# One more weight tile looked up on TensorE in the step loop of a one-core transformer layer

## The reference, cut to what matters

```
H, I, CS, CB = 1024, 2752, 8, 16384
Wg, Wu, Wd = codebook[idx_gate], codebook[idx_up], codebook[idx_down]   # (I,H), (I,H), (H,I)
g = einsum('bsh,ih->bsi', x, Wg)
u = einsum('bsh,ih->bsi', x, Wu)
out = einsum('bsi,hi->bsh', silu(g) * u, Wd)                            # x: (2, 1024, 1024)
```

## Time and profile before

| | us |
|---|---|
| median of 3 runs | 6918.13 |
| lowest and highest | 6914.07, 6921.35 |
| the profiled execution | 6914.47 |
| its span | 6912.6 |
| TensorE busy | 6672.6 (97%) |
| GpSimd busy | 5037.7 (73%) |
| VectorE busy | 4539.3 (66%) |
| ScalarE busy | 3665.4 (53%) |

### The profile page before, as it was taken

The page is one execution under the profiler, slowest core; times in us unless marked ns, Lnnn a source line. Parts: engine busy times, 40 slices in busy tenths (PEclk is TensorE's granted clock), DMA queues, the critical chain, the costliest instruction groups (busy, mean ns, idle before and its releaser), DMA issues.

```text
span 6912.6 us, 118754 instructions
## 1 busy us (share of the span) xinstructions
PE 6672.6 (97%) x29072; PEld 4082.8 (59%) x29072; DVE 4539.3 (66%) x11051; ACT 3665.4 (53%) x6498; POOL 5037.7 (73%) x5316
## 2 busy tenths in 40 slices
PE   9999999999999999999999999999999999999936
PEld 4444666666666566666666666666666666666513
DVE  3320778887777677776677766777767777677512
ACT  0000777776666555555555655555555555555401
POOL 7777777777777777777777777777777777777773
PEclk9999999999999999999999999999999999999968
DMA  4232111113333333333333333333333333333211
GB/s 139 61 89 47 33 34 34 34 34 89 81 84 82 62 67 73 72 73 73 67 74 73 73 74 73 66 73 74 73 73 67 77 73 72 74 68 73 59 13 51
DMA packets 472588, 463.19 MB, mean 67 GB/s; under 512 B 231248, under 2 KB 347728, under 8 KB 467536
## 3 DMA queue, kind: packets, MB, share of 16 engines
q10 hardware_dynamic: 287072, 396.63, 20.4%
q0 software_dynamic: 169984, 22.10, 7.8%
q1 hardware_dynamic: 14832, 36.84, 1.4%
HBM read 397.97 MB, written 57.15 MB: 66 GB/s over the span
## 4 chain that ended last, share of the span: by engine, by line
DMA 73%; issue 24%; POOLq 1%; POOL 1%; PE 1%; DVE 0%; ACT 0%; DVEq 0%
DMA raw<-in_codebook_dram,idx_sb 73%; POOLq L207 1%; POOL raw L208 1%; PE ps L465 0%; DVE small L1040 0%; PE ps L552 0%; ACT arena L845 0%; POOLq L196 0%; DVE small L1043 0%; DMA idx_sb<-in_idx_dram 0%; PE ps L545 0%; POOLq L217 0%; DVE small L1050 0%; DVE big L979 0%; ACT arena L729 0%
## 5 line engine op out<-in xcount | busy, mean ns | idle before, releaser
L208 POOL DMA_INDIRECT raw<-in_codebook_dram,idx_sb x5312 | 5037.5, 948 | 1796.1 <-DMA raw<-in_codebook_dram,idx_sb 1595.2
L987 DVE TENSOR_SCALAR_CACHE_REDUCE onehot<-arena,small 128x512 fp32r<-128x512 f32 x3685 | 2514.3, 743 | 1045.9 <-PE ps L419 998.6
L419 PE MATMUL ps<-onehot,table 128*128 128x512 f32 x11776 | 3123.7, 416 | 21.3 <-ACT onehot L757 17.7
L419 PEld LDWEIGHTS ps<-onehot,table 128*128 128x128 f32 x11776 | 2194.5, 188 | 864.6 <-issue 357.6
L753 ACT ACTIVATE onehot<-arena,small 128x512 fp32r<-128x512 f32 x2211 | 1434.3, 713 | 1113.9 <-PE ps L419 1076.6
L757 ACT ACTIVATE onehot<-onehot,small 128x512 fp32r<-128x512 f32 x2211 | 1425.3, 708 | 0.0
L447 PE MATMUL ps<-big,arena 128*128 128x512 f32 (+1 forms) x2816 | 1295.7, 597 | 124.3 <-DVE arena L971 123.4
L447 PEld LDWEIGHTS ps<-big,arena 128*128 128x128 f32 (+1 forms) x2816 | 515.5, 187 | 725.5 <-issue 577.1
L465 PE MATMUL ps<-arena 128*128 128x512 f32 (+1 forms) x1408 | 651.3, 599 | 2.1 <-ACT arena L729 1.1
L994 DVE SCALAR_TENSOR_TENSOR picked<-arena,small,ps 128x512 f32<-128x512 f16 x736 | 548.3, 745 | 153.3 <-PE ps L430 139.0
L979 DVE TENSOR_TENSOR big<-ps,big 128x512 f32<-128x512 f32 x704 | 486.3, 691 | 161.1 <-PE ps L465 151.4
(11 more groups left out here) (69 smaller groups left out, 2740.6 us busy)
## 6 DMA issues: line engine op xcount, KB each, us to landing
arena<-code_low ACTq DMA_DIRECT2D x738, 256.0 KB
arena<-code_high ACTq DMA_DIRECT2D x738, 128.0 KB
raw<-in_codebook_dram,idx_sb POOLq DMA_INDIRECT x5312
gathered_units<-raw SPq DMA_DIRECT2D x40, 512.0 KB
arena<-gathered_units ACTq DMA_DIRECT2D x20, 1024.0 KB
queries_keys<-arena ACTq DMA_DIRECT2D x16, 1024.0 KB, 4.0
arena<-queries_keys ACTq DMA_DIRECT2D x32, 512.0 KB
big<-in_xT_dram ACTq DMA_DIRECT2D x4, 2048.0 KB, 16.9
```

Source lines behind the costliest of these rows:

```text
L208: pool.indirect_dma_start(raw[:, s, n, :], None, codebook, bass.IndirectOffsetOnAxis(ap=idx_sb[:, s, n:n + 1], axis=0), engine_sem=describ ...
L419: last = mm(ps[:, 4 + s % 2, :], table[:, k, c, :], onehot[:, k, :], start=(k == 0 and c == 0), stop=(k == KLO - 1 and c == PIECES - 1))
L987: dve.tensor_scalar(onehot[:, k, :], lo_sb[:, s % 2, :], kp_sb[:, k:k + 1], None, ALU.is_equal, ALU.add, accum_out=hits[:, k:k + 1]).then_ ...
```

## The change

Down of tile 21 is looked up instead of gathered. NLOOK goes from 23 to 24 and the gathered units from 42 to 41; the step loop runs from 1 to 20 on every engine; behind it only gate, up and down of tile 21 are left, and the transposes of the gathered down weight go. The scratch areas for the codes are 3200 instead of 3072 wide. An index load for unit 41 is still issued, of zeros.

```diff
-NPK = NTILE - 1
-UNITS = 1 + 2 * (NTILE - 1) + 1
-PAIRS = (UNITS - 4) // 2
+UNITS = 1 + 2 * (NTILE - 1)
+PAIRS = (UNITS - 3) // 2
-NLOOK = 3 + NPK
+NLOOK = 3 + NTILE
@@ GpSimd
-            for s in range(2):
-                gather_unit(1, s, P, 16 * PAIRS + 32, 16 * PAIRS + 16, 2 * P * (PAIRS + 1) + (s * P - P + CS * CS))
+            gather_unit(1, 0, P, 16 * PAIRS + 32, 16 * PAIRS + 16, 2 * P * (PAIRS + 1) + (CS * CS - P))
@@ TensorE
-            with pe.Fori(1, NPK) as step:
+            with pe.Fori(1, NTILE) as step:
                 lookup_step(step, P, step * SLOTS + 3 * SLOTS, step + 3)
             fold(NLOOK - 1, QUADS - 1)
             for n in range(2 * CS * NT):
-                ffn_matmul(NPK, P, n)
-            pe.wait_ge(gu_in, NPK * 16)
-            pe.wait_ge(masked, NLOOK * SLOTS)
-            for r in range(4):
-                if r >= 2:
-                    pe.wait_ge(w_ready, NPK * 4 + 4 + (r - 1))
-                turn_weights(r // 2, r % 2, 4 + r % 2)
-            for n in range(2 * CS * NT, 3 * CS * NT):
-                ffn_matmul(NPK, P, n)
-            for n in range(2 * CS * NT):
                 t, rest = divmod(n, 2 * CS)
                 gate_up(NTILE, P, t, rest // CS, rest % CS)
-            pe.wait_ge(gathered[1][1], 16 * P * (PAIRS + 2 - PAIR_CUT))
-            last_d = raw[:, 1, :, :].rearrange("p (h j) e -> p h (j e)", h=CS)
-            for h in range(CS):
-                last = nc.tensor.transpose(...)
-            last.then_inc(turn_done, 1)
@@ ScalarE
-            with act.Fori(1, NPK) as step:
+            with act.Fori(1, NTILE) as step:
                 lookup_step(step, P, step + 3)
-            act.wait_ge(down_done, NPK * 32)
+            act.wait_ge(lo_in[1], NLOOK * SLOTS * 8 + 16)
+            for b in range(2):
+                act.wait_ge(hi_in[b], NLOOK * SLOTS * 4 + 16)
+                act.sem_inc(act_passed, 1)
+            act.wait_ge(down_done, NTILE * 32)
             take(NLOOK - 1, d_rep)
-            act.wait_ge(w_ready, NPK * 4 + 4)
-            load_gate_up(2 * NPK - 1, NPK)
-            for t in range(NT):
-                gate(NPK, P, t)
-            for r in range(4):
-                unpack(NTILE, r)
             for t in range(NT):
                 gate(NTILE, P, t)
-            turned(2, P, 4)
@@ VectorE
-            with dve.Fori(1, NPK) as step:
+            with dve.Fori(1, NTILE) as step:
                 lookup_step(step, P, step + 3)
-            for t in range(NT):
-                hidden(NPK, P, t)
-            for d in range(CS * NT):
-                add(NPK, d)
```

More of the change, by code:

```diff
@@ L80, in seq_post_ln_layer @@
         sem = lambda name: ctx.enter_context(nc.semaphore(name))
-        units = nc.dram_tensor("gathered_units", (UNITS - 1, P, P * CS), F32)
+        units = nc.dram_tensor("gathered_units", (UNITS, P, P * CS), F32)
         lo_dram = nc.dram_tensor("code_low", (NLOOK + 1, SLOTS, N), F32)
@@ L138, in seq_post_ln_layer @@
         cb_top = big2[:, 0, 1024:1024 + KLO * NHI * CS]
-        prep = lambda n: big2.rearrange("p e s -> p (e s)")[:, S + n * 3 * N * 2:S + n * 3 * N * 2 + W_CODE]
+        prep = lambda n: big2.rearrange("p e s -> p (e s)")[:, S + n * W_CODE:S + (n + 1) * W_CODE]
         code, lo_int, hi_int, lo_f = prep(0).bitcast(I32), prep(1).bitcast(I32), prep(2).bitcast(I32), prep(3)
@@ L150, in seq_post_ln_layer @@
         kp_sb, hi_row_sb = small[:, 25:25 + KLO], small[:, 33:34]
-        pool_passed = sem("pool_passed"); dve_passed = sem("dve_passed"); pe_passed = sem("pe_passed")
+        pool_passed = sem("pool_passed"); dve_passed = sem("dve_passed"); pe_passed = sem("pe_passed"); act_passed = sem("act_passed")
         idx_in = [sem(f"idx_in{s}") for s in range(2)]
@@ L254, in _ @@
                     store_unit(1, s, 2 * p + s, P, 16 * P * p - 16 * P * (PAIR_CUT - 1), 16 * p + 16, True)
-            store_unit(1, 0, UNITS - 2, P, 16 * P * (PAIRS + 2 - PAIR_CUT), 16 * PAIRS + 32, False)
+            store_unit(1, 0, UNITS - 1, P, 16 * P * (PAIRS + 2 - PAIR_CUT), 16 * PAIRS + 32, False)
             for k in range(SB):
@@ L454, in down @@
                 if d == 0:
-                    if isinstance(step, int) and step in (0, NTILE):
-                        pe.wait_ge(d_ready, 1 + step // NTILE)
+                    if isinstance(step, int) and step == 0:
+                        pe.wait_ge(d_ready, 1)
                     else:
@@ L526, in _ @@
             for n in range(2 * CS * NT):
-                ffn_matmul(NPK, P, n)
-            pe.wait_ge(gu_in, NPK * 16)
-            pe.wait_ge(masked, NLOOK * SLOTS)
-            for r in range(4):
-                if r >= 2:
-                    pe.wait_ge(w_ready, NPK * 4 + 4 + (r - 1))
-                turn_weights(r // 2, r % 2, 4 + r % 2)
-            for n in range(2 * CS * NT, 3 * CS * NT):
-                ffn_matmul(NPK, P, n)
-            for n in range(2 * CS * NT):
                 t, rest = divmod(n, 2 * CS)
                 gate_up(NTILE, P, t, rest // CS, rest % CS)
-            pe.wait_ge(gathered[1][1], 16 * P * (PAIRS + 2 - PAIR_CUT))
-            last_d = raw[:, 1, :, :].rearrange("p (h j) e -> p h (j e)", h=CS)
-            for h in range(CS):
-                last = nc.tensor.transpose(ps[:, 4 + h // 4, (h % 4) * P:(h % 4 + 1) * P], last_d[:, h, :], id_sb[:, :])
-            last.then_inc(turn_done, 1)
             def turn_y(k):
@@ L719, in unpack @@
                 act.copy(w_rep[:, m, 4 * h:4 * h + 4, :],
-                         ps[:, 4 + r % 2 if isinstance(step, int) else 3, :].rearrange("p (k n) -> p k n", k=4)
+                         ps[:, 3, :].rearrange("p (k n) -> p k n", k=4)
                          ).then_inc(w_ready, 1)
@@ L1092, in lay_out_indices @@
     j0 = HALF // CS
-    idx = np.zeros((UNITS, P, P), gate.dtype)
+    idx = np.zeros((UNITS + 1, P, P), gate.dtype)
     idx[0, :, 0:CS * j0] = down[:, :, 0:j0].transpose(1, 0, 2).reshape(P, CS * j0)
@@ L1098, in lay_out_indices @@
         idx[2 * t - 1], idx[2 * t] = gate[rows[t]], up[rows[t]]
-    idx[UNITS - 1] = whole[NTILE - 1].transpose(1, 0, 2).reshape(P, P)
     first = [w.reshape(P, CS, JT).transpose(1, 0, 2)
@@ L1103, in lay_out_indices @@
     codes[0:NLOOK] = [w.reshape(2, 4, P, QUAD, JT // QUAD).transpose(0, 4, 3, 1, 2).reshape(2, JT, 4, P)
-                      for w in first + whole[0:NPK]]
+                      for w in first + whole]
     return idx, codes.reshape(P, W_CODE)
```

## The result

The changed kernel takes 6884.69 us (median of 6 runs, 6878.02 to 6887.78), the kernel before, measured in the same rounds, 6916.20 us: 31.5 us less, ratio 0.9952 with a 95% interval of 0.9939 to 0.9965, which is 24 to 42 us. The profiled execution took 6884.99 us, its span 6883.2 us, against 6914.47 and 6912.6.

A forecast was written before the change was run, and what follows sets the result against it. TensorE was taken to bound the step loop and gathers the end, leaving it 165.4 us idle. 213.7 + 11.8 + 2.3 + 55.2 = 283.0 against 312.0 us, 2.2 less behind: 31.2 less, 6887 us, range 6875 to 6900.

The forecast's parts named there:

- The extra step and its stall: Step loop's end: one more full step costs 213.7 us, plus 11.8 us waiting and 2.3 us of low clock.
- The release R: ScalarE's slot 20, last step: the load waiting for unit 40 can go at 6677.0, bounds 6675.6 to 6680.0.
- The stall: Last step, slot 21: TensorE waits for ScalarE's one-hot tiles queued behind the late load; step 11.8 us longer.
- The clock: Behind TensorE's wait in the last step: a short piece at 1.2 GHz costs 2.3 us, ends 0 and 2.3.
- Behind the loop: 55.2 us of tile 21's gate and up without gap; the last down batch, starting warm, gives back 2.2 us.
- (a): Last step: TensorE doesn't wait, so 11.8 and 2.3 us go: 6873 us; chance 0.09.
- (b): Last step: the remaining 11 slots also wait for code loads, 17 us more: 6904 us; chance 0.10.
- (c): After TensorE's wait: clock stays at 1.2 GHz, 129 us more: 7013 us; chance 0.05.
- (d): End of the kernel: gathering still ends last, so nothing is gained: 6918 us; chance 0.02.

The follow-up runs named there:

- drop41: Kernel before without the 128 gathers of unit 41, TensorE transposing whatever is in the buffer (wrong result): 6875.11 us, ratio 0.9936.
- gates_first: Kernel before with ScalarE's four activations of tile 20 ahead of the load of tile 21's gate and up: 6923.21 us, ratio 1.0003.
- still_gathered: Changed kernel with unit 41 still gathered, by all-zero indices and read by nobody: 6894.39 us, ratio 0.9958 to the kernel before.
- load22_turn23: Changed kernel with the gate and up load in slot 22 instead of 20, transposes kept in slots 23 to 29: 6880.75 us, ratio 0.9944.
- after_b: Changed kernel repeated unaltered on the second of the two slow chips: 13037.23 us, ratio 0.9963 to the kernel before.
- after_again: Changed kernel repeated unaltered on the first of the two slow chips: 12983.44 us, ratio 0.9963 to the kernel before.
- short112: Changed kernel without gathering unit 40's last 16 columns (wrong result), on the first slow chip: 12964.02 us, ratio 0.9947 to the kernel before.

## Why the prediction was right, step by step

The forecast was 6887 us for the median, the result 6884.69; the sum said 31.2 us less, 31.5 was measured and 29.4 lies between the two profiled spans. That 31.2 and 31.5 agree to 0.3 us is luck, since the interval is 24 to 42 us and the medians of the kernel before differ by 2 us between the two measurements (6918.13 and 6916.20). What the traces can bear out is the working, term by term:

- **The extra step and its stall.** From the first gate matmul of before (6526.53) to that of after (6754.84) are 228.3 us; the sum had 213.7 + 11.8 + 2.3 = 227.8.
- **The release R.** Forecast 6677.0, measured 6677.51, but by another way. I had added 1.4 us for a later landing. It landed as fast as before (6674.69 - 6672.42 = 2.27 us, 2.37 before); the last gather itself was issued 2.0 us later than before (6672.42 against 6670.44). Two small errors cancelled, and the 0.5 us is luck: the same store was issued at 6668.03 (drop41), 6672.81 (before), 6676.78 (gates_first), 6674.69 (after), 6677.59 (still_gathered) and 6678.39 (load22_turn23), a scatter of 10 us, 8.8 of them among the three kernels in which TensorE stands idle beside the gathers. The bound of 6680.0 was too low: in load22_turn23 the load could only go at 6684.34, 5.95 us behind the store, and SyncE's longest wait for a store there was 5.4 us (5.0 in the changed kernel), more than the 4.4 that the bound was built on.
- **The stall.** Forecast 11.8 us, measured 12.20 in slot 21, in the place and by the engine that was named. That it hangs on ScalarE's position in the queue is shown by load22_turn23, that it hangs on the late unit by the runs where none is late.
- **The clock.** Taken as 2.3 us without a row for so short a stall. From the first of the six resumed matmuls to slot 22 are 5.94 us (6686.85 - 6680.91); one step earlier 6 of 16 matmuls and the three feed-forward ones took 3.6 us (6458.57, the start of the next look-up there, less 6452.35 + 10 x 0.264). That is 2.4 us.
- **Behind the loop.** 55.04 us to the first down (forecast 55.2). From there to the end of the span 73.32 us instead of 74.05: 0.7 us back where 2.2 were taken. The first batch of down alone did gain 2.0 us (15.37 against 17.35); 1.3 us went again behind it, where TensorE waits for ScalarE's layer norm and its clock rises and falls in both kernels: in the 25 us behind the first batch the granted clock was 0.86 on average, 0.93 in the kernel before. Why it fell lower isn't shown. The same stretch, from the first down matmul of tile 21 to the end, takes 72.07 us in drop41, 72.25 in still_gathered, 73.38 in after_b and 74.44 in after_again, which all reach it warm, and 74.96 in gates_first, which reaches it cold like the kernel before. So the 2.2 us could not be told from its scatter. This is the one mis-sized term, and with the 0.5 us of the first point it makes the 1.8 us between 31.2 and 29.4 up to rounding.
- **The rivals.** (a) no stall: refuted by the 12.20 us. (b) slow slots after the stall: from slot 22 (6686.85) to the last fold TensorE is busy for 67.10 of 67.10 us. (c) the clock stays low: 1.00 from 6686.90 on. (d) the gathers still end last: GpSimd's last work is at 6672.42 of 6883.2.

That 165 us of idle time were worth only 31 was in the sum and is now shown by three numbers: of the waits, only the 41.9 us for unit 41 was on the path (drop41, 45 less); moving 21 of the 123 us away was worth nothing (gates_first); and the filled kernel is held by the next limit, TensorE's own work plus 15 us of a unit that is late.

## What to carry to other kernels

Add up idle time only where a wait ends the path: here a 123 us wait was worth nothing as long as one of 42 us came behind it, and one reordering run and one run without the work told them apart. When work is moved from a slow stream to the engine that idles beside it, the gain is the distance to the next limit, so find the wait that the new step inherits, and what is queued behind it on the same engine. A wait for a late producer belongs as far back in an in-order queue as its consumer allows; here two slots later took the stall from 12.2 to 1.7 us, though the producer came 6.8 us later.

## What the runs showed of the hardware that was not expected

Two of the three chips used for variants run this program in 13 ms instead of 6.9. The page of the changed kernel there (after_again; 40 slices of the span, then two groups of instructions with the idle time before them):

```profile
PE   4666522122221222122121499999999999999999
...
POOL 6666666666666666666666400000000000000000
PEclk6766655555555555555555699999999999999999
...
L207 POOL DMA_INDIRECT raw<-in_codebook_dram,idx_sb x5184 | 4934.5, 952 | 2402.2 <-issue 2151.6
...
L607 ACT COPY arena<-ps 128x512 f32<-128x512 f32 (+3 forms) x768 | 347.7, 482 | 4739.3 <-remote 3987.8
```

```profile
1000.00:7300.00 6300.00, 1559.35 (x5873) 739.80 (x5871) 471.17 (x1084) 468.49 (x1087) 4229.52 (x4455) 0.53 0.10 11
7340.00:7730.00 390.00, 379.27 (x3640) 256.92 (x3636) 293.55 (x720) 282.74 (x719) 0.00 (x0) 0.98 0.13 39
```

The second fence has windows of the same trace: length, busy us of PE, PEld, DVE, ACT, POOL, then TensorE's granted clock, the DMA share and GB/s. As long as GpSimd gathers, TensorE is busy for 25% of the time (1559 of 6300 us), in projection and attention code that keeps it at 99% in the trace of the first chip (1118.5 of 1125 us), and the idle time of the engines has no releaser within the program ("issue", "remote"). In the window that begins 4 us behind the last gather it is back at 97%. A gather costs about 1.42 us there (7336.1 / 5184), 1.29 in the changed kernel's first trace (6672.42 / 5184), and single instructions last no longer (952 and 949 ns). So a gather's price is not a constant of the kernel: on such a chip the other engines get through the same code at about a quarter of the pace as long as gathers run, so that every gather delays them too.

By the medians the change gains 45.1 and 45.2 us there instead of 31.5, although nothing waits for unit 41; the intervals overlap. An estimate fits that: if nothing waits for a unit in either kernel, the change adds 268.9 - (312.0 - 165.4) = 122.3 us of TensorE's work behind the loop of before, so a gain of 45 us needs 167 us from 128 gathers, 1.3 us each, about what a gather takes there. Sixteen fewer (short112) took 19.4 us off the median, 1.2 us each, but 10.3 us off the profiled span, with overlapping intervals. No trace of the kernel before was taken on such a chip. What starves the engines is not shown. The instruction queues moved as much there (239 and 482 packets, 3.92 and 3.95 MB) as on the first chip, so more instruction loading is not it; slower instruction delivery beside the gathers would fit, and was not tested.
